# The hyperbolic attention as one program instead of two: projections and the unit loop interleaved, spike logits as two more columns of v's projection, q and k scaled in place

## The reference, cut to what matters

```python
importance = sigmoid(x @ w_sur + b_sur); spikes = importance > threshold
q, k, v = (x @ W_qkv + b_qkv).reshape(B, T, 3, H, D).transpose(2, 0, 3, 1, 4)
def expmap0_split(u):                       # of q and of k
    mink = -u[..., :1] ** 2 + sum(u[..., 1:] ** 2)
    nomin = sqrt(maximum(mink, 1e-8))
    return cosh(nomin), sinh(nomin) * u[..., 1:] / nomin
neg_inner = tq * tk - sq @ sk.T
scores = -arccosh(maximum(neg_inner, 1 + 1e-7)) ** 2 / sqrt(D)
attn = softmax(causal(scores)) * spikes
y = (attn @ v) @ W_out + b_out
```

## Time and profile before

| what | value |
|---|---|
| median of 3 runs | 2069.12 us (2066.55 to 2072.94) |
| profiled execution | 2071.58 us, span 2069.8 us |
| PE, DVE, ACT, POOL busy | 93%, 69%, 53%, 41% of the span |
| first program of the hyperbolic attention | 1114.2 to 1168.4 us |
| second program | 1169.2 to 1285.6 us |

### The profile page before, as it was taken

One profiled execution on the slowest core, in us unless ns is written; L12 is line 12 of the kernel. 1 busy time (PEld: TensorE's weight loads), 2 busy tenths in 40 slices (PEclk: granted clock), 3 DMA queues, 4 the chain that ended last, 5 costly groups with the idle time before them and its releaser, 6 DMA issues. The chain is left out here.

```text
span 2069.8 us, 35351 instructions
## 1 busy us (share of the span) xinstructions
PE 1923.5 (93%) x12240; PEld 1620.3 (78%) x12240; DVE 1434.9 (69%) x2398; ACT 1105.4 (53%) x2118; POOL 849.8 (41%) x854
## 2 busy tenths in 40 slices
PE   8999999999999999999998677999999768959998
PEld 6788888888888888888887465788799646849998
DVE  7777676767767676776776896433589577857776
ACT  6555555545555554555544697232355365636664
POOL 7350321405032140504200185220399225968885
PEclk9999999999999999999999799999999779969999
DMA  4101010010101001010102201310156215556661
GB/s 155 62 1 62 1 61 0 20 41 0 61 0 61 0 23 37 0 61 0 29 1 62 62 3 42 123 41 11 63 192 211 65 26 148 185 204 209 213 214 45
DMA packets 96322, 144.51 MB, mean 70 GB/s; under 512 B 15358, under 2 KB 72608, under 8 KB 96096
## 3 DMA queue, kind: packets, MB, share of 16 engines
q1 hardware_dynamic: 89168, 127.21, 19.1%
q0 software_dynamic: 4928, 12.86, 1.8%
q10 hardware_dynamic: 2128, 3.15, 0.4%
HBM read 111.46 MB, written 14.16 MB: 61 GB/s over the span
## 5 line engine op out<-in xcount | busy, mean ns | idle before, releaser
L319 PE MATMUL ps<-cond_x_lo,cond_w_hi 128*128 128x512 f32 x1008 | 392.6, 389 | 0.0
L471 ACT ACTIVATE cond_h_hi<-cond_h 128x512 fp32r<-128x512 f32 x288 | 174.0, 630 | 289.7 <-DVE cond_h L666 289.6
L805 POOL TENSOR_TENSOR cond_w_lo<-cond_stage_up,cond_w_hi 128x512 fp32r<-128x512 f32 x36 | 47.1, 1308 | 591.8 <-ACT cond_w_hi L471 591.8
L319 PE MATMUL ps<-cond_x_hi_first,cond_w_hi 128*128 128x512 f32 x578 | 230.1, 398 | 3.1 <-DVE ps L652 2.5
L382 PE MATMUL ps<-cond_h_hi,cond_d_hi 128*128 128x512 f32 x576 | 224.8, 390 | 4.1 <-DVE cond_h_lo L671 4.1
L319 PE MATMUL ps<-cond_x_hi_first,cond_w_lo 128*128 128x512 f32 x578 | 225.2, 390 | 0.0
L382 PE MATMUL ps<-cond_h_hi,cond_d_lo 128*128 128x512 f32 x576 | 224.3, 389 | 0.0
L382 PE MATMUL ps<-cond_h_lo,cond_d_hi 128*128 128x512 f32 x576 | 224.2, 389 | 0.0
L319 PEld LDWEIGHTS ps<-cond_x_lo,cond_w_hi 128*128 128x128 f32 x1008 | 189.3, 188 | 37.2
L649 DVE TENSOR_TENSOR ps<-cond_p_row,ps 128x512 f32<-128x512 f32 x142 | 98.7, 695 | 170.7 <-PE ps L319 170.7
L524 ACT ACTIVATE cond_h<-ps 128x512 f32<-128x512 f32 x216 | 124.7, 596 | 164.8 <-DVE cond_h_lo L671 132.2
(11 more groups left out here) (427 smaller groups left out, 5122.4 us busy)
## 6 DMA issues: line engine op xcount, KB each, us to landing
moe_stage_up<-in_L_ffn_expert_wv SPq DMA_DIRECT2D x22, 1024.0 KB, 7.9
typed_stage_up<-in_L_cond_wi SPq DMA_DIRECT2D x11, 1024.0 KB, 5.0
typed_stage_dn<-in_L_cond_wo SPq DMA_DIRECT2D x11, 1024.0 KB
moe_stage_dn<-in_L_ffn_expert_proj SPq DMA_DIRECT2D x11, 1024.0 KB
cond_stage_up<-in_L_cond_Wg SPq DMA_DIRECT2D x7, 1024.0 KB, 5.1
cond_stage_up<-in_L_cond_Wu SPq DMA_DIRECT2D x7, 1024.0 KB, 7.2
cond_stage_dn<-in_L_cond_Wd SPq DMA_DIRECT2D x7, 1024.0 KB, 9.5
rope_v_now<-rope_v_blk SPq DMA_DIRECT2D x16, 272.0 KB, 2.4
```

The source lines that it names most:

```text
L319: ins = pe.matmul(bank, ws[:, j, u, w], xs.rearrange("p o n -> p (o n)"), start=(opens and k == 0), stop=(k == 2), skip_group_check=True)
L471: copy = lambda dst, src: act.activation(dst, src, ACT.Copy)
L805: return pool.tensor_tensor(w_lo[:, j, :, A11:A12 + 1], raw_up[:, :, :, upper(j)], w_hi[:, j, :, A11:A12 + 1], ALU.subtract)
```

## The change

There is one program. PE, ACT and DVE run through the projections of tiles 0 to 15, and from tile 12 on the steps of the units are put behind each projection: step u = i - 11 follows the projection of tile i (`DELAY` = 11). Steps 5 (`AFTER`) to 25 follow alone. The phases, their lags and their order within a step are as before.

- The norms are made for tiles 0 to 6 (`FIRST` = 7) between the projections of tiles 7 to 10, and for tiles 7 to 15 in steps 5 and 6 of the units: parts 0 to 3. The reciprocal and one of the two operations on the first feature are gone: the first feature becomes half the cosh, and `stretch` multiplies only the other 15 features of each head, in place.
- w_sur stands twice as a column behind v's weights, b_sur behind v's bias. v's matmuls have 258 columns, and the 128 matmuls are gone. ACT takes the exponential after each fourth tile, and eight DMAs move the 16 columns of spikes to the rows of the units.
- The first source piece is 128 tokens wide, so that PE can begin earlier.
- ACT's `block_values` for the last tiles and its second `exponentials` stand inside the units' steps 4 to 7.
- The projections write banks 4 to 7. Several buffers lie over others that are done with, and so the 2 MB of x come back (`x_saved`) only after the last projection.

```diff
@@ hyper_attention: one block; PE
-                    for i in range(NP):
-                        for sq in range(4):
...
-                                ins = pe.matmul(m.bank[7][row:row + T // 2, i:i + 1], srcT[:, k, token:token + T // 2], ws[:, k:k + 1],
-                                                start=(k == 0), stop=(k == KC - 1))
+                def unit_steps(u):
+                    units(u, (out, 9), (mix, 8), (score, 3), (p_turn, 7), (y_turn, 8), (turn, 1))
+
+                for i in range(NP):
+                    project(i)
+                    unit_steps(i - DELAY)
+                for u in late_steps:
+                    unit_steps(u)
@@ ACT
+                for tt, start, stop in pieces[0:3]:
+                    round_src(tt, start, stop)
...
+                    if i % SUB == SUB - 1:
+                        act.wait_ge(v_taken, i + 1)
+                        act.activation(sig[:, tt * SUB:(tt + 1) * SUB], v_row[:, tt % 2, :, D], ACT.Exp, scale=-1.0).then_inc(sp_small, 1)
...
+                    if i == FIRST + 1:
+                        exponentials(0)
+                    unit_steps(i - DELAY)
...
+                for u_step in late_steps:
+                    unit_steps(u_step)
+                    if u_step == AFTER:
+                        exponentials(1)
+                        block_values(TT - 2, 1)
+                    elif u_step == AFTER + 1:
+                        block_values(TT - 1, 0)
+                    elif u_step == AFTER + 2:
+                        block_values(TT - 1, 1)
@@ DVE
-                        link(dve.reciprocal(below[:, at], ser[:, at]))
-                        dve.scalar_tensor_tensor(first[:, :, 0:H], cosh[:, at, 0:H], -1.0, below[:, at, 0:H], ALU.mult, ALU.mult)
-                        dve.tensor_tensor(first[:, :, H:], cosh[:, at, H:], below[:, at, H:], ALU.mult)
+                    dve.tensor_scalar(firsts(at), cosh, 0.5, None, ALU.mult).then_inc(spaced, 1)
...
                 def stretch(i, q):
 
-                    wait(dve, turned, i - 1)
-                    dve.tensor_tensor(x[:, q].rearrange("p (h d) -> p h d", d=DH), qk[:, i].rearrange("p (h d) -> p h d", d=DH),
-                                      space[:, i].unsqueeze(2).to_broadcast([P, 2 * H, DH]), ALU.mult).then_inc(stretched, 1)
+                    dve.wait_ge(spaced, 2 if i < FIRST else 4)
+                    space_of = heads(qk[:, i])[:, :, 1:]
+                    dve.tensor_tensor(space_of, space_of, space[:, i].unsqueeze(2).to_broadcast([P, 2 * H, DH - 1]), ALU.mult)\
+                        .then_inc(stretched, 1)
...
+                space_norm(NP - 1)
+                norms(1, 0)
+                for u_step in late_steps:
+                    unit_steps(u_step)
+                    if u_step == AFTER:
+                        norms(1, 1)
+                        norms(1, 2)
+                    elif u_step == AFTER + 1:
+                        norms(1, 3)
+                        spikes()
@@ SP
+                sp.wait_ge(v_done, NP)
+                sp.dma_start(resT[:].rearrange("p c n -> p (c n)"), m.x_saved).then_inc(m.x_back, 16)
+                sp.wait_ge(sp_steps, 3)
...
+                        sp.dma_start(spike[sq * S:(sq + 1) * S].rearrange("p (i q) -> p i q", q=2)[:, :, q],
+                                     sig[row:row + S].rearrange("p (i a) -> p i a", a=2)[:, :, sq // 2],
+                                     allow_slow_non_contiguous=True).then_inc(spike_moved, 16)
```

More of the change, by code:

```diff
@@ L1279, in __init__ @@
             self.loads += [(to[:, :, c, r], of[:, :, r, c]) for c, r in blocks]
-        self.loads.append((self.wq[:, :, QK:], rows(w_qkv)[:, :, QK:]))
+        self.loads.append((self.wq[:, :, QK:3 * D], rows(w_qkv)[:, :, QK:]))
+        if b_qkv is not None:
+            self.loads += [(self.wq[:, :, 3 * D + j], col(w_sur)) for j in range(2)]
         self.loaded, self.rounded, self.ready = (ctx.enter_context(nc.semaphore(f"{tag}_weights_{name}"))
@@ L1360, in hyper_units @@
     causal = [m.const[:, at:at + n].unsqueeze(1).to_broadcast([P, H, n]) for at, n in zip((C_FIRST, C_SECOND), keys)]
[L1361 to L1367, removed]
-    sem = StageSemaphores(nc, tag)
-    stretched, turned, k_turned, q_taken, k_blocked = (
-        sem(n) for n in ("stretched", "turned", "k_turned", "q_taken", "k_blocked"))
+    sem = StageSemaphores(nc, tag)
+    src_rounded, src_ready = sem("src_rounded"), sem("src_ready")
+    qk_done, v_done, qk_taken, v_taken = sem("qk_done"), sem("v_done"), sem("qk_taken"), sem("v_taken")
+    v_doubled, v_blocked, ones_set = [sem(f"v_doubled{i}") for i in range(2)], sem("v_blocked"), sem("ones_set")
+    sp_small, sp_steps, spike_moved = (sem(n) for n in ("spike_exp", "spike_steps", "spike_moved"))
+    squared, made, norm_act, norm, spaced = (sem(n) for n in ("squared", "made", "norm_act", "norm_steps", "spaced"))
+    bias_joined = sem("bias_joined")
+    stretched, turned, k_turned, q_taken, k_blocked = (sem(n) for n in ("stretched", "turned", "k_turned", "q_taken", "k_blocked"))
     scored, clamped, root_squared, root_logged, rooted = (
@@ L1393, in hyper_units @@
         wide = lambda a, q: by_head(a[:, q], q)
+        pieces = [(0, 0, P), (0, P, TW)] + [(tt, 0, TW) for tt in range(1, TT)]
+        late_steps = range(AFTER, NP + 10)
         def wait(eng, s, count):
@@ L1527, in p_take, with unit_steps @@
                     act.activation(pT[:, q].rearrange("p h n -> p (h n)"), pT_ps, ACT.Copy).then_inc(p_taken, 1)
-                run(act, "scalar", dict(q_blk=lambda i, q: take_q(act, copy, i, q), y_take=lambda n, q: take_y(act, copy, n, q),
-                                        root_sq=root_square, root_ln=root_log, root=root, dist_ln=dist_log, dist=dist,
-                                        prob=exponential, p_take=p_take))
+                def unit_steps(u):
+                    units(u, (root_log, 4), (dist, 5), (root_of, 4), (p_take, 7), (exponential, 6), (take_q, 1),
+                          (root_square, 3), (dist_log, 4))
@@ new lines, in norms @@
+                def norms(n, part):
+                    at = GROUPS[n]
+                    sm, ser, inv, ep, en, cosh = (a[:, 0:COUNTS[n]] for a in (sms, sers, invs, eps, ens, coshs))
+                    if part == 0:
+                        under_root(n, at, sm, ser)
+                    elif part == 1:
+                        series(sm, ser)
+                    elif part == 2:
+                        sinh(n, sm, ser, inv, ep, en)
+                    elif part == 3:
+                        choose(at, sm, ser, ep, en, cosh)
+                        time_and_space(n, at, ser, cosh)
@@ L1599, in shift, with unit_steps @@
                                        ALU.subtract).then_inc(shifted, 1)
+                def unit_steps(u):
+                    units(u, (mask, 5), (root_add, 4), (shift, 5))
+                column = v_blk[:].rearrange("p i j g h v -> p (i j g) h v")[:, :, :, DH]
+                pool.tensor_copy(column, half2.unsqueeze(1).to_broadcast([P, NP * 2 * HP, 2])).then_inc(ones_set, 1)
+                for u_step in range(0, AFTER):
+                    unit_steps(u_step)
+                pool.wait_ge(src_ready, TT + 1)
```

479 lines of the change are left out of this document (222 added, 257 removed).

## The result

The changed kernel takes 2082.84 us (median of 4 runs, 2079.58 to 2083.79), the kernel before in the same comparison 2069.01 (4 runs). The ratio is 1.0063, with a 95% interval of 1.0047 to 1.0079: slower by 10 to 16 us, and outside the range that was given. The profiled execution after is the quickest of the four, 2079.58 us with a span of 2077.8.

A forecast was written before the change was run, and what follows sets the result against it. Projections were taken as bound by PE, the middle by DVE's chain and latencies, the units by ACT. On the 2069.12 us median, -0.2 + 1.2 = +1.0 gave 2070.1, own range 2065 to 2075, whole range 2059 to 2078.

The forecast's parts named there:

- the sixth, "At nothing": Wider v matmuls, weights' loads, x's return, stretch and spike DMAs: all costed at nothing; the spikes had the thinnest cover.
- Step 1: Start of the attention: a smaller first source piece lets PE begin earlier, 1.45 us gained.
- Step 2: Norms 0 between tiles 7 and 10: DVE's work ends at 1150.05, PE pauses some 3 us before turn 0.
- Step 3: Tiles 13 to 15 take 5.2 us each instead of 2.2; root_ln(0) comes 13.1 us earlier.
- Step 4: Units' steps 4 to 7 give the gain back: root_ln(4) at 1199.15 against 1199.37, 0.2 us left.
- the first rival: Units' steps 4 to 7 are looser, bounded by ACT's own work: about 2061.6 us, faster; chance 0.28.
- Step 5: PE's clock after the pause before turn 0: tile 13 alone at half clock, 1.2 us lost.
- the second rival: PE's clock stays half through tiles 13 to 15 and DVE waits for POOL: 2077.7 us, slower; chance 0.17.
- The third rival: Spikes or x come late, so scale_y(0) and ACT behind it wait: +6 us, 2076, slower; chance 0.05.

The follow-up runs named there:

- e1: The kernel before with 192 bytes left free behind the attention's weights, nothing else changed: 2080.91 us, ratio 1.0048 to before.
- e4: The changed kernel with 64 bytes left free behind the attention's weights, so the experts' buffers lie 256 bytes beyond before: 2069.80 us, ratio 0.9996 to before.
- e8: The changed kernel with 64 bytes free, second exponentials, parts 1, 2 and the sums of part 3 of the second norms left out: 2062.92 us.
- e7: The changed kernel with 64 bytes free and, on DVE, top(0) ahead of second norms' parts 1 and 2, part 3 later, spikes earlier: 2068.16 us.

## Why the prediction was wrong, step by step

**The step that failed is the sixth, "At nothing": the weights' "1540 for 1536 columns".** I costed the extra columns as work and as loads, and both are nothing, as said. What they cost is the place of all that is reserved behind them: 10.84 us, in a stage that I had taken as fixed. e1 and e4 show this from both sides. No row of before could show that price, but that buffers move could be read from the code, and neither the sum nor a rival had it. With the place put right (e4) the changed kernel takes 2069.80, where 2070.1 was forecast. That the two are so near is partly luck: before took 2071.65 in that comparison. What holds is the ratio of 0.9996, 0.9984 to 1.0009, no difference that can be told.

**Step 1, the start.** PE begins 1.35 us after the rounding, against 2.46 before: 1.1 gained instead of 1.45. DVE's rest of the first piece took 0.76 us, not the 0.41 that I took from a sum of the same 256 elements.

**Step 2, norms between tiles 7 and 10.** Right. On the clock of before (10.84 taken off) DVE's work ends with the first stretch at 1150.7, forecast 1150.05; PE pauses for 2.35 us, forecast some 3.

**Step 3, 5.2 us for a tile.** Right: additions 13 to 15 are 5.10 and 5.23 apart. root_ln(0) is 12.2 us earlier than before, against 13.1 less the 1.2 of the clock.

**Step 4, all given back.** Right in sum and in its places: 33.62 us from root_ln(0) to root_ln(4), forecast 34.5; top(0) 15.8 after root_ln(0), forecast 16.0; ACT idle for 8.9 of them, forecast some 10. root_ln(4) is 0.2 us earlier than before in the stage, and 0.5 later in e4. The loop through DVE is what binds, as e8 shows. What I had wrong is that this must be so: I gave the first rival, with its gain of 8.5 us, a chance of 0.28, as part 2 can't begin before the exponentials. That is true of part 2, but top needn't stand behind it, and e7 gets 4.6 us of it.

In parts 1 and 3, DVE's first operation took 2.26 and 2.14 us instead of 0.46, and the next of part 3 took 1.41. Each ended 0.3 us after the operation of POOL beside it, and together they took 4.4 us more than alone (forecast 3.1). By the rule of the Trainium skill (SBUF — State Buffer, "SBUF: two separate sides"), an operation of VectorE with two SBUF inputs and one of GpSimd that reads SBUF lock one port pair against each other. The trace agrees for these norms as for the stretch, and the 2.5 us that would have come back without it did not.

**Step 5, the clock.** 0.78 and 0.88 in the two windows behind turn 0, so part of one tile at half, as taken. Over the 17 us of the second rival (1161 to 1178 here) the granted clock was 0.90, and its bound was under 0.6.

**Step 6, the rest of it.** x landed in 7.9 us, at 1186.8, over 20 us ahead of its use. The spikes landed in 1.9 (median of eight); the last did so at 1206.56, and DVE needed them at 1208.65. That cover of 2.1 us (forecast 0.8) held. The third rival fell.

**The stage as a whole.** -0.44 us in the profiled run and +1.3 in e4, forecast +1.0. Eight executions with the old stage took 171.1 to 173.4 us, mean 172.3, so the two of the new one, mean 172.6, can't be told from it. No gain and no loss of the change by itself can be told here, and the forecast of this part held.

**What stays open of the sum.** In the profiled executions the pieces add up to +8.0 us, the medians differ by 13.8. The piece behind the attention varies by some 4 us between executions (779.9 to 784.4), whatever the kernel, and the one profiled of after was its quickest. The medians of before in the other four comparisons were 2069.80 to 2071.65, so up to 2.6 us of the 13.8 may lie in the 2069.01 of this one.

## What to carry to other kernels

A wider tile moves every buffer that is reserved behind it. Before an edit of sizes is costed, compare the byte addresses of what TensorE reads in the other stages, and compare the rate of an untouched stage first when the result is known. Where a batch of work is put into a pipelined loop, put it behind the operation that the other engines wait for: here the same work lengthened the stretch from root_ln(0) to root_ln(4) by 7.4 us ahead of top and by 2.8 behind it.

## What the runs showed of the hardware

- In the first mixture, back-to-back matmuls of 128x512 (fp32r) started 227.4 ns apart where the moving tile and the weights of all of them agreed in their address modulo 256 bytes, 230 to 231 where a quarter disagreed, 231.6 where three quarters did, and 233.3 where all did, at a granted clock of 1.00 throughout. These are means of about 1040 starts. It is at most 2.6%, but in a stage that TensorE bounds it all comes through. In the attention's projections the place counts too, but agreement did not make two of three forms quick (233.0 and 233.6 ns in e1).
- With 256 columns the same projections show no order by agreement: their starts were 115.5 to 117.0 ns apart where the tiles disagree (before, 22 of each form) and 117.0 to 120.0 where they agree (e1).
- The profile shows this neither as a wait nor as a lower clock: PE stays busy for 100%. Only the count in a window and the mean of a group tell.
- A one-input operation of VectorE (L1742, 288 elements) also took 2.51 us in e7, against 0.43 in e8, and ended 0.3 us after an addition of POOL; so not only operations with two inputs are held up.

```profile
1188.54 2.51 DVE L1742 TENSOR_SCALAR hyp_qk<-hyp_cosh 128x288 f32<-128x288 f32 x1
```

```profile
1188.15 2.60 POOL L1848 TENSOR_TENSOR hyp_z<-hyp_z,hyp_t 128x1024 f32<-128x1024 f32 x1
```
